# Three sixteen-head attentions: row maxima split and later groups normalised on GpSimd, output projections added in pairs

## The reference

```python
x = x + attention(_layernorm(x), ctx_1024, ctx_1024, Wq, Wk, Wv, Wo)

def attention(Q, K, V, ...):                 # 32 entries of 128 tokens, 128 columns
    q, k, v = (Q @ Wq.T), (K @ Wk.T), (V @ Wv.T)      # split into 16 heads of 8
    scores = einsum('bhqd,bhkd->bhqk', q, k) / sqrt(8)
    ctx = einsum('bhqk,bhkd->bhqd', softmax(scores), v)
    return ctx @ Wo.T
# A1 rotates q and k (rope); A2 has biases, and one k and v head shared by all 16
```

## Time and profile before

| | before |
|---|---|
| median of 3 runs | 1471.62 us (1470.96 to 1475.32) |
| span of the profiled execution | 1467.0 us |
| the runs' median less that span | 4.6 us |
| loops of A0, A1, A2 in the profile | about 55 to 231, 566 to 781 and 858 to 1036 us |
| VectorE busy / TensorE busy over the span | 67% / 80% |

### The profile page before, as it was taken

How to read it: one execution, slowest core, us unless ns; L and a number is a source line. 1 busy time by engine, 2 the same in 40 slices (tenths; PEclk the granted TensorE clock), 3 DMA queues, 4 the chain that set the end, 5 groups by cost and what they waited for, 6 DMA issues and landing times. The chain is left out here.

```text
span 1467.0 us, 34935 instructions
## 1 busy us (share of the span) xinstructions
PE 1171.7 (80%) x11141; PEld 918.1 (63%) x11154; DVE 988.9 (67%) x2920; ACT 667.1 (45%) x1423; POOL 538.9 (37%) x590
## 2 busy tenths in 40 slices
PE   2699994439999957779987879999799956499991
PEld 1477773338899925556673456677477755399991
DVE  3689996474443347998984679888477777766552
ACT  1367762105555503345564546766234343144440
POOL 2324201664235256534411232431121125752554
PEclk9999997559999967899998989999799988599996
DMA  6887743012223258435532177564200042133542
GB/s 179 206 215 191 188 124 129 29 33 87 77 92 109 75 133 209 122 101 144 150 84 51 44 176 167 150 163 106 86 1 0 0 152 74 53 120 106 149 140 73
DMA packets 138978, 164.58 MB, mean 112 GB/s; under 512 B 15308, under 2 KB 118754, under 8 KB 131728
## 3 DMA queue, kind: packets, MB, share of 16 engines
q1 hardware_dynamic: 130664, 146.62, 37.0%
q0 software_dynamic: 8192, 16.46, 4.1%
HBM read 111.98 MB, written 51.38 MB: 111 GB/s over the span
## 5 line engine op out<-in xcount | busy, mean ns | idle before, releaser
L586 DVE TENSOR_REDUCE A_neg_max<-A_s_bank 128x4 f32<-128x512 f32 x384 | 253.2, 688 | 46.3 <-PE A_s_bank L725 35.9
L448 ACT ACTIVATE A_probsT<-A_st_bank 128x512 f32<-128x512 f32 x384 | 222.4, 602 | 40.4 <-PE A_st_bank L738 39.2
L725 PE MATMUL A_s_bank<-A_k_stack,A_q_stack 72*128 72x128 bf16 x1536 | 157.5, 228 | 38.0 <-DVE A_neg_max L586 22.3
L738 PE MATMUL A_st_bank<-A_q_stack,A_k_stack 128*128 128x128 bf16 x1536 | 153.1, 224 | 7.1 <-DVE A_q_stack L602 6.2
L738 PEld LDWEIGHTS A_st_bank<-A_q_stack,A_k_stack 128*128 128x128 bf16 x1536 | 112.5, 103 | 52.2 <-issue 42.9
L725 PEld LDWEIGHTS A_s_bank<-A_k_stack,A_q_stack 72*128 72x128 bf16 x1536 | 106.3, 102 | 52.1 <-DVE A_neg_max L586 33.4
L752 PE MATMUL A_pv_bank<-A_probsT,A_v_pad 128*32 128x128 f32 x3072 | 127.4, 284 | 1.5 <-issue 1.5
L2041 ACT ACTIVATE E_h<-E_h_bank,w_L_b 128x256 f32<-128x256 f32 x184 | 76.8, 471 | 72.4 <-PE E_h_bank L2141 71.0
L2153 PE MATMUL E_y_bank<-E_w,E_h 128*128 x736 | 90.3, 276 | 2.2 <-ACT E_h L2041 0.9
L752 PEld LDWEIGHTS A_pv_bank<-A_probsT,A_v_pad 128*32 128x32 f32 x3072 | 74.1, 111 | 24.7 <-issue 3.4
L2141 PE MATMUL E_h_bank<-E_xT,E_w_u 128*128 128x256 f32 x368 | 88.8, 386 | 0.0
(11 more groups left out here) (371 smaller groups left out, 2641.4 us busy)
## 6 DMA issues: line engine op xcount, KB each, us to landing
A_q_stack<-q_scratch SPq DMA_DIRECT2D x48, 576.0 KB
A_k_stack<-k_scratch SPq DMA_DIRECT2D x32, 576.0 KB
q_scratch<-A_q_parts SPq DMA_DIRECT2D x48, 192.0 KB, 2.3
A_k_stack<-k_scratch SPq DMA_DIRECT2D x48, 192.0 KB
E_xe<-slots_in SPq DMA_DIRECT2D x53, 128.0 KB, 2.1
slots_out<-E_ye SPq DMA_DIRECT2D x53, 128.0 KB, 1.7
A_ctxT<-in_ctxT SPq DMA_DIRECT2D x24, 256.0 KB, 10.5
k_scratch<-A_k_parts SPq DMA_DIRECT2D x32, 192.0 KB
```

The costliest lines, as they stand in the source:

```text
L448: act.activation(probsT[n % 2][:, c * HQ:(c + 1) * HQ, :], st_bank[c % 2][:, :].rearrange("k (a q) -> k a q", a=HQ), ACT.Exp, scale=scale) ...
L586: dve.tensor_reduce(neg_max[:, c * HQ:(c + 1) * HQ], s_bank[c % 2][:, :].rearrange("q (a k) -> q a k", a=HQ), AX.X, ALU.max, negate=True). ...
L725: last = pe.matmul(s_bank[c % 2][:, a * S:(a + 1) * S], q_stack[slot][0:COMBO, h, at:at + S], k_stack[slot][0:COMBO, h, at:at + S], start= ...
L738: last = pe.matmul(dst, k_stack[slot][:, h, at:at + S], q_stack[slot][:, h, at:at + S], start=True, stop=spread)
```

## The change

- `split_max` for entries 2 to 31 goes from DVE to GpSimd. For that `neg_max` has two buffers. GpSimd's program is now written entry by entry: in iteration b it splits the maxima of b+2 first, and then does the group's work: `split_rest` of k at b%4 = 1, of q at b%4 = 2 (with the bias in A2), and at b%4 = 3 the inverse deviation and `normalise` of group g+3. A1's late rows are issued behind the split of iterations 0 to 4.
- `normalise` of groups 3 to 7 goes from DVE to GpSimd, in all three attentions three groups ahead; `mv` has two buffers. A1 takes the statistics in two halves, as A0 and A2 did.
- `add_x` becomes `add_pair`: projections of two entries lie side by side in `wo_bank`, and every second iteration one instruction of 256 columns adds both. The transposed maxima have columns of their own, so that `transpose_max` waits for an addition only in every second iteration.

```diff
+    NORM_AHEAD = 3
+    STATISTICS = {0: range(0, 2), 2: range(2, GB)}
...
+            def normalise(g):
+                pool.wait_ge(rstd_done, g + 1)
+                pool.wait_ge(prep_ready, U * (g - 1) + X + 1)
+                core.settle(pool)
+                for j in range(GB):
+                    last = pool.tensor_scalar(xn[:, j, :], core.x_tile(g * GB + j), mv[g % 2][:, j, 0:1],
+                                              rstd[:, j:j + 1], ALU.subtract, ALU.mult)
+                last.then_inc(xn_done, 1)
+
+            def split_max(b):
+
+                pool.wait_ge(max_done, 4 * (b + 1))
+                pool.wait_ge(mt_ready, b)
+                core.settle(pool)
+                own.link(pool.tensor_copy(max_parts[:, hi:hi + NH], neg_max[b % 2][:, :]))
+                core.settle(pool)
+                pool.tensor_tensor(max_parts[:, lo:lo + NH], neg_max[b % 2][:, :], max_parts[:, hi:hi + NH], ALU.subtract)\
+                    .then_inc(m_split, 1)
+                pool.wait_ge(m_split, b + 1)
...
+            inverse_deviation(2)
+            for b in range(NB):
+                g = b // GB
+                if has_scores(b + 2):
+                    split_max(b + 2)
+                if late:
+                    late_rows(*{0: (7, 10), 1: (10, 11), 2: (11, 12), 3: (12, 13), 4: (13, 16)}.get(b, (0, 0)))
+                if b % GB == 1 and exists(g + 2):
+                    split_rest(pool, own, k_f, k_parts, kd, g + 2, KL, k_lead, k_split)
+                if b % GB == 2 and exists(g + 2):
+                    split_rest(pool, own, q_f, q_parts, D, g + 2, QL, q_lead, q_split)
+                    add_bias(g + 2)
+                if b % GB == 3 and exists(g + 3):
+                    inverse_deviation(g + 3)
+                    normalise(g + 3)
...
-            def add_x(b, n=0):
-
-                if shared_kv and n % GB == 1:
-                    dve.wait_ge(bias_added, add_x.it * 2 + n // GB + 1)
+            def add_pair(b, n=0):
+
+                if shared_kv and n % GB == 2:
+                    dve.wait_ge(bias_added, add_pair.it * 2 + n // GB + 1)
                 dve.wait_ge(wo_ready, START + b + 1)
-                dve.tensor_tensor(core.x_tile(b - 1), core.x_tile(b - 1), wo_bank[:, 0:D], ALU.add)\
+                dve.tensor_tensor(core.x_pair(b - 2), core.x_pair(b - 2), wo_bank[:, 0:2 * D], ALU.add)\
                     .then_inc(x_added, 1)
...
-                    add_x.it = it
-                    add_x(b, n)
-                    if has_scores(b + 2):
-                        split_max(b + 2)
+                    if n % 2 == 0:
+                        add_pair.it = it
+                        add_pair(b, n)
                     place(1)
```

More of the change, by code:

```diff
@@ L653, in _ @@
                 spread_max(0, 0)
[L654 to L656 removed]
+            statistics(2, 0)
+            normalise(2)
             def late_result(i):
```

142 lines of the change are left out of this document (54 added, 88 removed).

## The result

The changed kernel takes 1477.99 us (median of 20 runs, 1472.01 to 1483.39) against 1471.68 (20 runs, 1465.73 to 1479.42) before: a ratio of 1.0037, 95% interval 1.0022 to 1.0052. It is slower by about 5 us, where 6 us faster was forecast. The medians of before beside the later experiments are 1471.34, 1471.78, 1475.62 and 1470.6, so what follows compares the ratios; 0.1% is 1.5 us.

What follows compares the result with a forecast made beforehand. In the attention loops PE and DVE were both taken as near full, so DVE relief was worth only PE's waits for it. A0 - 2.5, A2 - 4.5, A1 + 1 gave - 6 us: 1466 us, range 1455 to 1483.

Steps and rivals of the forecast that it cites:

- my terms of 0.5 and 0.9: Gain per group from PE waiting less for DVE: 0.5 us in A0, 0.9 in A2, in five groups each.
- The narrow pair: Cast and subtraction of the split on GpSimd: 0.2 us each, split's end 0.76 us after the last maximum.
- The last entries: A0's final entries, without group work: 4.66 us each, forecast to stay so.
- The 0.34 us to spare: Slack of the split before PE transposes the maxima, read in A0's final entries; the split was to come 0.15 us later.
- the second rival: GpSimd's split ends late and slows every entry, if above 0.95 us after its last maximum: 1482 us, chance 0.24.
- four pieces that I put at 0.35 each: GpSimd's normalisation of a group, 0.35 us per instruction; with inverse deviation and gaps 2.9 us.
- makes it 4.8: In A2, split_rest with the bias behind it takes GpSimd 4.8 us, called close.
- I let the two cancel: Shared port: split's leaving saves up to 0.8 us an entry, but DVE's copy meets more GpSimd work; net nothing.
- 6.6 us in entries of 6.15: In A1, GpSimd's k or q split plus the maxima's split, twice running, against the entry length.
- one wait of 1.5 us a group: A1: maxima late behind q's split, 1.5 us; less 0.75 of relief, + 0.75 in each of four groups.
- The first entries gained nothing where I took 2 us: A1's first eight entries, DVE-bound: relieved of 5.2 us, of which 2 us was counted as gain.
- the sum had + 1: A1 in total: + 3 us from four steady groups, less 2 us in the first entries, + 1 us.

Runs made afterwards that it cites:

- e7: Kernel before with only the normalise moved to GpSimd; split on DVE, x added tile by tile: 1463.6 us, ratio 0.9947.
- e11: e4 with the last two steps of each q split in A0 and A2 held until DVE's spreading copy is done: 1492.7 us, ratio 1.0136.
- e4: Changed kernel with GpSimd's normalise cut in two, two tiles in a group's last entry, two in the next entry: 1474.8 us, ratio 1.0034.
- e2: Changed kernel with only the split of the maxima back on DVE: 1463.7 us, ratio 0.9967.
- e6: Kernel before with only x added in pairs and the transposed maxima moved in the PSUM bank: 1470.9 us, ratio 0.9993.
- e12: Kernel before with the split of the maxima on GpSimd, inverse deviation queued ahead of the q split: 1485.2 us, ratio 1.0103.
- e1: Changed kernel with normalise back on DVE, two tiles in each of two entries of the following group: 1477.8 us, ratio 1.0052.
- e3: Changed kernel with both split and normalise back on DVE, pair addition and moved maxima kept: 1476.4 us, ratio 1.0037.

## Why the prediction was wrong

The time lies in the range of 1455 to 1483, but on the other side of no change than the forecast of 1466.

**Bound and DVE's relief: right in kind.** Groups of A0 and A2 do shorten when DVE is relieved. e7 takes 1.37 us a group from DVE (4 x 0.34) and shortens four groups by 2.2 us in A0 and 2.1 in A2, 0.5 each, beside my terms of 0.5 and 0.9; A1's steady groups stay (96.4 against 96.2). DVE was put a little too full: 112.19 and 110.88 of 125 us are 90 and 89%, and without what overlaps it is 88% of A0's loop. With the loops' first entries it is worth 8 us (0.9947), where the whole change was to bring 6.

**The narrow pair: right.** 0.20 and 0.22 us, gap 0.18, the split's end at 0.75 to 0.79 us behind the last maximum where GpSimd is free, forecast 0.76. The last entries stay at 4.66, and in A0's steady groups PE did not come to wait for stacks.

**What the pair's time was held against: not so in the loop.** The 0.34 us to spare, and with them the second rival's 0.95 us, were read in the last entries, which have no group work. The loop's entries have other room. Before, in A0, a row of the loop:

```profile
131.58 0.17 DVE L595 TENSOR_TENSOR A_max_parts<-A_neg_max,A_max_parts 128x16 bf16<-128x16 f32 x1
131.81 0.10 PEld L761 LDWEIGHTS A_wo_bank<-ident,A_max_parts 128*128 128x128 bf16 x1 [0.38 <-DVE A_max_parts L595]
```

Here PE follows 0.06 us behind the split, having waited; in two of a group's four entries nothing is to spare, as the two waits of the earlier trace rows say too. In e11's entry above lateness counts from 0.79 us on and not from 0.95.

**First step that failed: "four pieces that I put at 0.35 each".** They are 0.79 where undisturbed, 0.89 in the mean. Inverse deviation and normalisation take 127.81 to 133.02, 5.2 us, not 2.9. With the split ahead of them they outlast an entry. With 0.35 they would have fitted. That mistake is 0.65 us a group in A0: e4, which does the same work in two pieces, gets 2.6 us back in four groups. In A2 a second sum was short: the bias "makes it 4.8" leaves the pair's 0.76 us out, with which GpSimd's work takes 5.6 us and more. From the last maximum at 931.64 us to the end of the bias addition at 937.75 it took 6.1, in an entry of 4.9 us, as the four entries of a group are not equally long. I had interpolated by columns between a narrow tensor_scalar and a cast, but the cast has no per-partition operands, and the bound above, the 1.16 us of a 128x512 subtraction, I did not carry.

**Second: "I let the two cancel".** The port was weighed as a matter of amounts. What counted was phase. The split's move puts GpSimd's q split, in A0 and A2, behind the maxima and its last step on top of a copy: 0.57 us in that entry, 0.58 in the next one's length. The copies went from 727 to 834 ns in the mean, 10 us in sum, and back to 731 in e2, where only the split is back. The normalisation, the new work, hardly lengthens them: of the 13.7 us by which the changed kernel's copies exceed 0.69 us each, 0.4 stand beside it. What those 10 us cost in time is not read off; the nearest figure is the 1.9 us of A0's four steady groups between e4 and e2.

**Third: A1.** The queueing was foreseen (6.6 us in entries of 6.15), its price was not. I had one wait of 1.5 us a group, half paid by DVE's relief; the trace has two, 0.99 and 1.91 us, and the lowered clock behind the second. The steady groups went from 96.2 to 103.3, 1.8 a group, instead of 0.75. The first entries gained nothing where I took 2 us. The last four gave 3.2 us back (19.5 us instead of 22.7): before, PE waits 2.8 us for the last stack there, and now 0.8, since it comes later. So the loop as a whole is 4.0 us longer in the kept traces, where the sum had + 1. A small slip stands in that sum: addition and split take 0.58 us by its own rows, not 0.67.

**In sum** the steady groups are 2.1, 7.1 and 3.0 us longer in A0, A1 and A2, where the sum had - 2, + 3 and - 3.6 for four groups. By the ratios normalise alone is - 8 us (e7), pairs alone - 1, which is nothing measurable (e6), and the split alone + 15, of which some 4 may be that version's own wait (e12), and + 10 on top of the other two (changed kernel against e2). The three single parts add up to + 6, and + 5 was measured, so within the intervals the parts add. The direction was wrong because the move that was counted as relief of DVE, 0.4 us an entry, is one whose result PE waits for, put behind the queue of an engine that does long work. My rival of the late split had the right mechanism; it was priced as an offset in every entry and not as collisions in some of them. The time lies inside the stated range by luck, since the upper end stood on that pricing. What the changed kernel's first entries add is not settled, nor are e1's and e3's times, whose steady A0 and A2 are as in before.

## What to carry to other kernels

A short instruction on the critical ring must not share a queue with long ones, however idle that engine is on average: compare the longest run of its other work with the shortest time between two due dates, because in the entries shown lateness was paid one for one. Read what there is to spare in the entries that have the other work, not in quiet ones. Work with no due date in the entry, like the normalisation, is what to move: alone it gave 0.5%. When work is moved between VectorE and GpSimd, look at what it displaces, and whether that now meets a long copy on the other engine; and test the parts of a change one by one, since a part that gains 8 us can stand beside one that loses 10 or more.

## What the runs showed of the hardware

- GpSimd's tensor_scalar with two per-partition operands took 0.79 us for 128x128 in f32, 2.3 times the 0.34 on DVE, while its subtraction of four times the columns took 1.16. Columns alone don't give the price.
- A DVE copy of 32x2048 bf16 that begins while a GpSimd subtraction of 128x512 is under way ended 0.55 us after it in the cases shown (0.69 alone, up to 1.70). GpSimd's instruction is stretched if it begins second: in e2 the first step of the k split, 0.29 us behind the start of a copy, took 1.42 us instead of 1.16. That agrees with the Trainium skill ("SBUF — State Buffer", rules for kernel authors), by which the later of the two waits. e4's copy at 128.36 looks like an exception, as it took 0.69 us although GpSimd was normalising from 127.65 for 2.07 us; but those are two pieces, the first ending 0.09 us after the copy's start, and the second, which begins behind it, took 1.28 us instead of 0.79.
- The order of the rows does not always tell who waits. In the changed kernel a piece of the normalisation that starts at 940.88, 0.25 us ahead of DVE's copy, took 1.14 us instead of 0.79, and the copy 0.74. That does not fit the rule just named, if the starts of the rows are taken as they stand.
